# A decoder layer on one core: second norm left unwritten, weights folded in four parts, three buffers for two

## The reference

```python
qf, kvf = fft(heads(x @ W_q.T)), fft(heads(x @ W_kv.T))      # 16 heads of 16
qf, kvf = qf / norm(qf), kvf / norm(kvf)
a  = real(ifft(qf * cumsum(kvf, over tokens))) @ W_o.T
x1 = layernorm(x + a)
x2 = layernorm(x1 + causal_mha(q=x1, k=ctx, v=ctx))          # 16 heads, softmax
w  = ternary(weight, 0.2, 0.6) + rram_variation
x3 = layernorm(x2 + ternary(x2, 0.33, 0.5) @ w.T)
```

## Time and profile before

| | |
|---|---|
| runs | 152.79, 153.93, 154.58 us; median 153.93 |
| profiled execution | 154.16 us, span 152.4 us |
| granted TensorE clock | 0.993 of full |
| instructions | 4763 |
| busy | TensorE 135.7, VectorE 131.9, ScalarE 115.5, GpSimd 100.5 us |

### The profile page before, as it was taken

One profiled execution on the slowest core, in us unless ns is written; L12 is line 12 of the kernel. 1 busy time (PEld: TensorE's weight loads), 2 busy tenths in 40 slices (PEclk: granted clock), 3 DMA queues, 4 the chain that ended last, 5 costly groups with the idle time before them and its releaser, 6 DMA issues.

```text
span 152.4 us, 4763 instructions
## 1 busy us (share of the span) xinstructions
PE 135.7 (89%) x1737; PEld 91.5 (60%) x1737; DVE 131.9 (87%) x420; ACT 115.5 (76%) x318; POOL 100.5 (66%) x212
## 2 busy tenths in 40 slices
PE   6999999999999799999999989999897988996540
PEld 2944657455674447766575856776675867674330
DVE  0036999999989699998999989999998999999972
ACT  3126655777694687979998999989999799978940
POOL 4020252536856457757989789799999889998542
PEclk9999999999999999999999999999999999999997
DMA  3897962231159404453283226845469951202212
GB/s 101 269 245 263 308 227 42 102 77 63 39 148 237 138 0 137 123 158 75 36 224 105 52 52 137 282 127 176 106 201 125 178 144 22 69 4 69 75 69 71
DMA packets 25208, 19.33 MB, mean 127 GB/s; under 512 B 13152, under 2 KB 21088, under 8 KB 25184
## 3 DMA queue, kind: packets, MB, share of 16 engines
q1 hardware_dynamic: 25184, 19.02, 47.5%
HBM read 14.16 MB, written 2.10 MB: 107 GB/s over the span
## 4 chain that ended last, share of the span: by engine, by line
PE 42%; DVE 22%; POOL 9%; SPq 7%; ACT 6%; issue 6%; DMA 5%; POOLq 0%
PE p L823 11%; DVE x L2101 8%; PE p L877 5%; PE p L843 5%; PE p L870 4%; POOL probs L418 4%; DMA x1T_b<-x_b 3%; PE p L897 3%; SPq L198 3%; POOL rstd L412 3%; PE p L829 3%; PE p L794 2%; ACT probs L1462 2%; PE p L799 2%; PE p L853 2%
## 5 line engine op out<-in xcount | busy, mean ns | idle before, releaser
L418 POOL TENSOR_SCALAR_AFFINE_SELECT probs<-probs 128x512 f32<-128x512 f32 x64 | 41.2, 663 | 8.6 <-ACT probs L1462 7.9
L2101 DVE TENSOR_REDUCE x<-p 128x4 f32<-128x512 f32 x64 | 41.7, 679 | 2.3 <-PE p L853 2.3
L1462 ACT ACTIVATE probs<-p 128x512 f32<-128x512 f32 x64 | 34.9, 602 | 4.3 <-PE p L870 4.2
L823 PE MATMUL p<-w_in,xT_s 128*128 128x512 f32 x64 | 30.2, 601 | 0.0
L412 POOL TENSOR_TENSOR rstd<-ve,power 128x1 f32<-128x1 f32 x48 | 27.6, 577 | 2.8
L1480 ACT ACTIVATE dev<-r,neg 128x256 f32<-128x256 f32 x41 | 21.0, 515 | 2.4 <-DVE neg L2074 2.4
L877 PE MATMUL p<-probs,vals 128*32 128x128 f32 x512 | 19.5, 278 | 0.7 <-ACT probs L1462 0.3
L870 PE MATMUL p<-x1T,keys 32*128 32x128 f32 x512 | 18.8, 283 | 1.0 <-ACT yT_s L1450 0.4
L870 PEld LDWEIGHTS p<-x1T,keys 32*128 32x128 f32 x512 | 15.7, 186 | 5.7 <-DVE x L2101 2.1
L407 POOL TENSOR_SCALAR ve<-spread 128x1 f32<-128x1 f32 x48 | 10.2, 212 | 13.1 <-ACT dev L1480 10.0
L823 PEld LDWEIGHTS p<-w_in,xT_s 128*128 128x128 f32 x64 | 11.4, 190 | 10.2 <-issue 9.1
(11 more groups left out here) (81 smaller groups left out, 252.2 us busy)
## 6 DMA issues: line engine op xcount, KB each, us to landing
keys<-ctxK SPq DMA_DIRECT2D x16, 256.0 KB, 3.6
vals<-ctxV SPq DMA_DIRECT2D x16, 256.0 KB, 3.2
xT_s<-xT SPq DMA_DIRECT2D x16, 128.0 KB, 3.0
x_s<-x SPq DMA_DIRECT2D x16, 128.0 KB, 3.2
out<-res SPq DMA_DIRECT2D x16, 128.0 KB, 2.3
wq_s<-w_q SPq DMA_DIRECT2D x1, 256.0 KB, 2.7
wkv_s<-w_kv SPq DMA_DIRECT2D x1, 256.0 KB, 3.8
fv_s<-ffn_vT SPq DMA_DIRECT2D x1, 256.0 KB, 3.4
```

The source lines that it names most:

```text
L418: nc.gpsimd.affine_select(out=part, in_=part, compare_op=ALU.is_ge, fill=0.0, base=0, pattern=[[0, GH], [1, TOK]], channel_multiplier=-1). ...
L823: last = nc.tensor.matmul(p[PROJ[n]][:], xT_s[n % XR][:, g, :], w_in[:, g, :], start=(g == HALVES[0]), stop=(g == HALVES[1]))
L1462: nc.scalar.activation(probs[n % 2][:, c, :, :].rearrange("p g q -> p (g q)"), p[SCORES[n][c]][:], ACT.Exp, scale=HD ** -0.5).then_inc(exp ...
L2101: nc.vector.tensor_reduce(x1[n % X1R][:, c::GH, HD], p[APPROX[n][c]][:].rearrange("p (h k) -> p h k", h=GH), AX.X, ALU.max, negate=True).t ...
```

## The change

1. x2 is never written. A new `threshold` forms 0.33 times the standard deviation as 0.33 x variance x (1/root), `low_threshold` its negative counterpart shifted by the mean, both 128x1 on VectorE, once for each batch. `ternary_above` and `ternary` compare the second sum itself with these. `add_feed_forward` takes the second sum times 1/root in place of x2; the constant it leaves out is the same for all features of a row, and the third norm removes it. Second sums now stay in SBUF for all batches.
2. All work tiles come in threes (`RING = 3`), the second sum in fours; `res` stays at two.
3. The eight PSUM banks become one tensor with the same eight parts. Scores remain one bank for each call of `exponentials`. The tables of banks are new.
4. 30 of the 48 variances (10, 8 and 12 of the three norms) run on ScalarE, as Identity with scale 1/256 and bias eps.
5. `ternary_above` runs 12 times on GpSimd and 4 on VectorE (7 and 9 before). Ten results become seven on ScalarE, and six nine on VectorE; of 16 `normalise_x1` ScalarE has 14 (12 before). All 16 `copy_outT` are ScalarE's; one `copy_yT` and one `round_x1` move to VectorE. Twelve DMA transposes of ternary values (ten before) and four on TensorE.
6. The weights come as four quarters: kv's first with the Fourier table in one transfer on SyncE, kv's second and q's first from ScalarE's queue, ahead of its table load, and q's second on SyncE. They are folded into four banks and copied in four 256-column pieces, and the first projection is made in two halves, kv then q. Five warming matmuls and one filler stand for seven and two.
7. The order of calls on each engine is new throughout.

```diff
+XR, X1R, RING = 6, 6, 3
-            sp.dma_start(wq_s[:], halves(w_q)).then_inc(in_fold, 16)
-            sp.dma_start(dft_s[:], dft).then_inc(in_fold, 16)
-            sp.dma_start(wkv_s[:], halves(w_kv)).then_inc(in_fold_kv, 16)
+            sp.dma_start(first_s[:], kv_dft).then_inc(in_first, 16)
             load_xT(0)
+            sp.dma_start(wq_s[1][:], w_q[1]).then_inc(in_q[1], 16)
...
+            def project_half(n, k, ready):
+                cols = slice(k * DIM, (k + 1) * DIM)
+                for g in range(2):
+                    pe.wait_ge(ready[g], 1)
+                    last = nc.tensor.matmul(p[PROJ[n]][:, cols], xT_s[n % XR][:, g, :], w_in[:, g, cols],
+                                            start=(g == 0), stop=(g == 1))
+                return last
...
+            act.dma_start(wkv1_s[:], kv_1).then_inc(in_kv, 16)
+            act.dma_start(wq_s[0][:], w_q[0]).then_inc(in_q[0], 16)
...
+            def variance(n, i):
+                nc.scalar.activation(ve[i][n % RING][:], spread[i][n % RING][:], ACT.Identity, bias=eps[:], scale=1.0 / DIM).then_inc(ve_done_act[i], 1)
...
             def add_feed_forward(n):
-                nc.vector.scalar_tensor_tensor(out=residual(n, 2), in0=heads(x2[n % 2][:]), scalar=1.0,
+                nc.vector.scalar_tensor_tensor(out=residual(n, 2), in0=residual(n, 1), scalar=rstd[1][n % RING][:],
...
+            def threshold(n):
+                nc.vector.scalar_tensor_tensor(out=width[1][n % RING][:], in0=ve[1][n % RING][:], scalar=TH_X, in1=rstd[1][n % RING][:],
+                                               op0=ALU.mult, op1=ALU.mult).then_inc(width_done, 1)
+
+            def low_threshold(n):
+                nc.vector.scalar_tensor_tensor(out=low[1][n % RING][:], in0=width[1][n % RING][:], scalar=-1.0, in1=neg[1][n % RING][:],
+                                               op0=ALU.mult, op1=ALU.subtract).then_inc(low_done, 1)
...
-            def normalise_x2(n):
-                nc.vector.tensor_scalar(heads(x2[n % 2][:]), residual(n, 1), neg[1][n % 2][:],
-                                        rstd[1][n % 2][:], ALU.add, ALU.mult).then_inc(x2_done, 1)
...
             def ternary_above(n):
-                nc.vector.tensor_scalar(above[n % 2][:], x2[n % 2][:], TH_X, None, ALU.is_gt).then_inc(above_done, 1)
+                nc.vector.tensor_scalar(heads(above[n % RING][:]), residual(n, 1), neg[1][n % RING][:], width[1][n % RING][:], ALU.add,
+                                        ALU.is_gt).then_inc(above_done, 1)
...
             def ternary(n):
+                nc.vector.scalar_tensor_tensor(out=heads(xq[n % RING][:]), in0=residual(n, 1), scalar=low[1][n % RING][:], in1=heads(above[n % RING][:]),
+                                               op0=ALU.is_lt, op1=ALU.subtract).then_inc(xq_done, 1)
```

More of the change, by code:

```diff
@@ L56 @@
[L56 to L68, removed]
@@ new lines, in decoder_layer @@
+        above, xq = several("above", [128, DIM], bf16), several("xq", [128, DIM], bf16)
+        xqT_s = several("xqT_s", [128, 2, TOK], bf16)
+        res = ring("res", 2, [128, DIM])
+        total, neg, spread, width, low = ([several(f"{n}{i}_", [128, 1]) for i in range(3)] for n in ("total", "neg", "spread", "width", "low"))
+        dev = [several(f"dev{i}_", [128, DIM]) for i in range(3)]
+        ve, rstd, shift = ([several(f"{n}{i}_", [128, 1]) for i in range(3)] for n in ("ve", "rstd", "shift"))
@@ L129, in tile32, with two_banks @@
+        banks = bank("banks", [128, 8, CW])
+        p = [banks[:, b, :] for b in range(8)]
+        def two_banks(b):
+            return banks[:, b[0]:b[1] + 1:b[1] - b[0], :]
         def tile32(b, parts, width):
@@ new lines, in _ @@
+            round_x1(13)
+            exponentials(10, 3)
+            act.wait_ge(x1T_done, 12)
+            copy_x1T(11)
+            act.wait_ge(shift_done[0], 13)
+            normalise_x1(14)
+            act.wait_ge(neg_done[0], 16)
+            deviations(15, 0)
+            act.wait_ge(pv_done[3], 10)
+            copy_outT(9)
+            act.wait_ge(var[0], 16)
+            variance(15, 0)
+            act.wait_ge(scored, 12)
+            exponentials(11, 1)
+            exponentials(11, 3)
@@ new lines, in _ @@
+            dve.wait_ge(rsA_squared, 13)
+            half_step(12)
+            low_threshold(0)
+            dve.wait_ge(low_done, 1)
+            dve.wait_ge(above_done_pool, 1)
+            ternary(0)
+            refine_norms(12)
+            dve.wait_ge(cum, 12)
+            cross_products(11)
+            dve.wait_ge(out_done, 3)
+            invert_sums(2)
+            dve.wait_ge(rnA_done, 13)
+            unit_vectors(12)
+            dve.wait_ge(rstd_done[1], 2)
+            threshold(1)
@@ L2579, in _ @@
             row_max(12, 3)
+            negative_mean(15, 0)
+            row_max(12, 1)
             row_max(12, 2)
-            normalise_x2(7)
-            row_max(12, 0)
+            dve.wait_ge(rstd_done[1], 8)
+            threshold(7)
+            low_threshold(6)
+            dve.wait_ge(width_done, 8)
+            low_threshold(7)
+            row_max(12, 0)
+            dve.wait_ge(low_done, 7)
+            ternary(6)
+            dve.wait_ge(out_done, 10)
+            invert_sums(9)
@@ L2643, in _ @@
+            row_max(15, 0)
+            row_max(15, 2)
+            dve.wait_ge(added[1], 12)
+            negative_mean(11, 1)
+            dve.wait_ge(rstd_done[1], 11)
+            threshold(10)
+            ternary(9)
+            row_max(15, 3)
+            row_max(15, 1)
+            dve.wait_ge(width_done, 11)
+            low_threshold(10)
+            ternary_above(10)
             dve.wait_ge(ffn, 9)
-            dve.wait_ge(out_ready, 6)
             add_feed_forward(8)
-            dve.wait_ge(above_done_pool, 7)
```

3127 lines of the change are left out of this document (1556 added, 1571 removed).

## The result

The changed kernel takes 162.2 us in the median of four runs (160.42 to 163.69), the kernel before 153.78 in the four runs beside it (152.79 to 154.58): a ratio of 1.051, 95% interval 1.040 to 1.063. It is 8.4 us slower, outside the forecast range. The profiled execution took 163.69 us, 162.0 of it span. It is the slowest of the four, at a mean clock of 0.930 (the others 0.953 to 0.972), and the ratios, unlike the medians, leave out runs that lie more than 1.5% above the fastest of their kernel, as this one does.

The account below looks back on a forecast made before the run. No single engine was taken to bound the middle, four being nearly full. Norm 0, buffers -1.0, start -0.5 and -0.3, tail 0 gave -1.8 us: 153.93 to 152.1 us, range 149.3 to 155.8.

Parts of the forecast that it names:

- SyncE's queue: SyncE's transfer list: two more DMA transposes ahead of loads and stores cost 0, about 1 us if a load is late.
- VectorE's sum: VectorE without the second norm: 11.3 us out, 11.6 in, net +0.3 us (-4.5 to +3.1), costed at 0.
- Its own sign of being wrong: VectorE: the forecast is wrong if thresholds take 0.3 us or more; it took 0.213 each.
- The pointers: VectorE's ternary and add_feed_forward, 32 instructions: pointer scalars for immediates cost 0.08 us each, 2.5 in all, lower bound 0.
- GpSimd: GpSimd: 30 variances leave (6.4 us), five more comparisons at 0.856 come (+4.3), net -2.1 us.
- The sum for one batch's latency: One batch's chain from root to ternary: old and new forms within 0.1 us of each other, no latency won.
- ScalarE: ScalarE: 30 variances at 0.21 us (+6.3), about +5 us in all, mostly hidden; total near 120.5.
- Rival (b): ScalarE becomes the bound, over some 97% busy from 60 to 140 us: 155.6 us, chance 0.16.
- Rival (a): VectorE's small instructions blocked by GpSimd masks: a third take 0.58 us, +4.1 us, 156.2; chance 0.06.
- The start: Weights and first projection: it ends near 9.1 us instead of 9.66, gain 0.5 us (0 to 0.8), plus 0.3 VectorE idle.
- Buffers and order: Three work buffers, new order and PSUM banks remove waits for free buffers: 1.0 us gained, between 0 and 5.3.
- The tail: After VectorE's last row maximum: difference between 0 and +1.0 us, taken as 0, bounds -0.5 to +1.0.

## Why the prediction was wrong

**The failed step: SyncE's queue.** The prediction wrote "Two more DMA transposes enter SyncE's queue with their waits, ahead of loads and stores; with tiles loaded several batches ahead I cost them at 0, and at about 1 us if a load of values or keys is then late." It looked only at what the transposes could delay, not at what could delay them. SyncE's new list has eleven loads between the transposes of batches 0 and 1, where the kernel before had two; the earlier trace rows give 0.45 us for an issue, so 5 us of queue could have been read off. Measured: 3.65 us from data to issue, and 4.3 us (5.4 by the ratios) for moving two calls.

**What had no term: TensorE's clock.** The kernel before had 1.00 in all stretches but the last; the prediction took it as given. It fell to 0.50 after the waits, and fillers in the waits gave back 3.0 us with the transposes still late. The two gains are parts of one: the queue makes the wait, and the clock fell behind the wait.

Of the 10.1 us between forecast and measurement (152.1 and 162.2), 5.5 went with the queue mended and the fillers in (156.66). Of the other 4.6, 1.8 are the gain that was forecast, and 2.8 an excess over the kernel before whose cause is open.

**VectorE's sum, right in kind and short in size.** Forecast +0.3 (bounds -4.5 to +3.1), measured +3.2 us (135.1 for 131.9). Its own sign of being wrong came, thresholds of 0.3 or more (0.312), and VectorE's idle time from 20 to 140 us is 9.7 us where it should have fallen below 5. The small instructions cost 8.4, not 6.8: their medians are 0.156 and 0.152, their longest 0.70 and 0.59. The pointers cost 1.4 (`ternary` 0.5, `add_feed_forward` 0.9), less than the 2.5 taken. Not in the sum were `refine_norms` (0.203 to 0.315 us each, +1.8) and `half_step` (+0.6), unchanged instructions that take longer in the new order. Costed at 0, the norm alone came to 3.1 us in the old order. A sum whose upper bound is +3.1 on an engine at 95% should not have stood at 0 beside the gains.

**GpSimd.** The prediction took 0.856 for a form that the trace did not show, with no upper bound, although it raised VectorE's price for the same two pointers by 43%. With the same factor 0.856 becomes 1.23; measured 1.27. Its net was +3.4 us, not -2.1. The sum for one batch's latency has the same gap: it took VectorE's 0.51 for the comparison, though twelve of the sixteen ran on GpSimd at 1.27. What the form costs the kernel is not settled: at most the 3.9 us of the run with the immediate, part of which came before the first comparison, and 0.3 (157.88 to 157.55) once SyncE's order was mended.

**ScalarE.** A variance took 0.298, not 0.21; the engine's total, 120.6, came out as forecast (120.5) all the same: the times of its instructions add up to some 7 us more, but they overlap, and the busy time rose by 5.1. The Trainium skill, page ScalarE: Activation LUTs, section "What ACT_TABLE_LOAD costs", gives about 280 ns plus 0.833 ns an element for an activation with a pointer bias, an estimate of 0.281 us for one element; the 0.298 of the 30 rows agrees within 0.02. The nearest row of the trace, the accumulator read, was not the same kind. Rival (b) did not happen by its own condition: from 60 to 140 us ScalarE is 89% busy (71.36 of 80), not over 97. Moving the variances back cost 4.8 us more, with 64 waits added.

**Rival (a)**, small instructions blocked, happened as to its mechanism: ten of the 32 take 0.38 to 0.70 us, the rest about 0.15, and each of the ten ends within 0.03 us of the end of a GpSimd instruction. Two of them, with the mask beside each:

```profile
71.48 0.63 POOL L428 TENSOR_SCALAR_AFFINE_SELECT probs<-probs 128x512 f32<-128x512 f32 x1
71.53 0.59 DVE L2128 SCALAR_TENSOR_TENSOR low<-width,neg 128x1 f32<-128x1 f32 x1
...
119.05 0.63 POOL L428 TENSOR_SCALAR_AFFINE_SELECT probs<-probs 128x512 f32<-128x512 f32 x1
119.12 0.57 DVE L2123 SCALAR_TENSOR_TENSOR width<-ve,rstd 128x1 f32<-128x1 f32 x1
```

The masks end at 72.11 and 119.68, the low threshold and the threshold at 72.12 and 119.69. The ten hold 3.6 us above 0.153 each; against the forecast's 0.213, which had such hits in it, the 32 came to +1.6 us (8.4 for 6.8), not +4.1. Of the eight `refine_norms` and `half_step` that take 0.34 us or more, seven end within 0.05 us of a GpSimd instruction too. By the rule on shared ports in the Trainium skill, page SBUF — State Buffer, section "SBUF: two separate sides", of two such instructions the later one waits for the whole of the first; the trace agrees, by these rows.

**The start** was right as far as can be told: the first projection ends at 9.25 (forecast 9.1), and alone it gives 0.4 us (forecast 0.5 to 0.8), an amount whose interval includes 0.

**Buffers and order, -1.0.** No run isolates the three buffers. What the runs show is that the new order as a whole gains nothing: with queue and clock mended it is 2.8 us slower than the kernel before, with the norm either way. **The tail**, costed at 0, ran at half clock: a feed-forward takes 1.47 us at 150.30 in the chain, for 0.83. From the end of the last row maximum to the end of the span it is 24.6 us (21.9 in the kernel before, 22.7 with the fillers, at a clock of 1.00 from 140 to 146 us and 0.96 to 152). The sum there was also wrong in itself: what goes adds up to 4.7 us with the two comparisons "above" and what comes to 3.9 to 5.0, so the difference lies between -0.8 and +0.3, not 0 and +1.0.

**Still open:** what makes those 2.8 us. The profiled spans differ by 2.1: the last row maximum ends 1.3 us later (131.8 for 130.5), and the tail is 0.8 longer. The clock is out, with 0.990 to 0.996 in all six runs. The norm and the one further wait on SyncE's list gave nothing when they were changed, the norm with the reservation above. The candidates left are the waits for exponentials and row maxima near 38 us, the 2.0 us of VectorE's extra work that writing the norm leaves, the three buffers with the new banks, which no run isolates, and the shift of work between engines in a plan with 95% full engines.

## What to carry to other kernels

A hand-ordered queue that does no arithmetic belongs in the sum like an engine: for every DMA whose input is made on the chip, count what stands ahead of it between the moment its data is ready and its issue, and what is still in flight when it is issued. A wait of TensorE can cost its length and then time at the lower clock, as two of three did here, so look in the windows at the clock behind each new wait. And before a difference between two runs is put down to an edit, compare their traces up to the first instruction that the edit touches: here 1.5 us had already come by then. Price an unseen form by the ratio that its neighbours on another engine show, never by the form that it replaces.

## What the hardware showed that was not expected

GpSimd's 128x256 comparison takes 1.23 to 1.27 us with two pointer scalars and 0.87 to 0.89 with an immediate, on the same input. Ten VectorE instructions of one element a row, of a kind that takes 0.15 us elsewhere, took 0.38 to 0.70 and ended with the GpSimd instruction beside them. A DMA transpose issued behind eight loads in a row took 5.3 us to land, against 2.5 in the median. Fourteen matmuls for nothing made the changed kernel 3.0 us faster. Of one kernel, two runs took 3.2 us longer than the other two, at a lower mean clock. And two savings of 4.3 and 3.9 us came to 4.6 together.
